# Index columns copied by ScalarE in the first edge stage and the edge GRU, and a later load of target rows in the third layer

## What is computed

```python
h = relu(layernorm(x))
# L0, three times: mean over incoming edges of h[src], at dst
h = relu(h @ W_self.T + b_self + (segment_sum(h[src], dst) * inv_deg) @ W_neigh.T)   # no relu on the third
x = x + h
# L1: h = (mean_dst(h[src]-ea) @ W_O.T + mean_src(h[dst]-ea) @ W_I.T + h @ W_S.T + biases) / 3, batch norm
# L2: messages = segment_sum(h[src] @ W_msg.T + b_msg + emb[type], dst); h = gru_cell(messages, h)
# L3: agg = segment_sum((h @ W.T + b)[dst], src) / deg
```

## Time and profile before

| | |
|---|---|
| median of three runs | 6240.1 us |
| profiled execution | 6218.8 us |
| its span | 6217.1 us |
| mean granted TensorE clock | 0.838 of full |
| busy over the span | PE 75%, PEld 56%, DVE 65%, ACT 47%, POOL 61% |

### The profile page before, as it was taken

The page is one execution under the profiler, slowest core; times in us unless marked ns, Lnnn a source line. Parts: engine busy times, 40 slices in busy tenths (PEclk is TensorE's granted clock), DMA queues, the critical chain, the costliest instruction groups (busy, mean ns, idle before and its releaser), DMA issues. The chain is left out here.

```text
span 6217.1 us, 110999 instructions
## 1 busy us (share of the span) xinstructions
PE 4637.3 (75%) x24481; PEld 3476.5 (56%) x24651; DVE 4013.2 (65%) x15472; ACT 2945.0 (47%) x6694; POOL 3765.4 (61%) x4109
## 2 busy tenths in 40 slices
PE   3886946668998997734756656899999988865564
PEld 1564634445686686624655444786666654544564
DVE  4875844444684685634237757769999989974431
ACT  0585744443583584433211100548888875544200
POOL 0466666660570470075747750758888878867687
PEclk7997966679999998855878989559999999985687
DMA  3454545558888887845766679544544445534554
GB/s 98 144 193 126 180 151 178 182 174 308 298 289 305 308 291 255 291 143 158 256 207 123 125 135 253 151 140 170 172 170 171 170 149 156 164 98 147 133 101 73
DMA packets 744937, 1140.21 MB, mean 183 GB/s; under 512 B 106431, under 2 KB 427341, under 8 KB 744420
## 3 DMA queue, kind: packets, MB, share of 16 engines
q1 hardware_dynamic: 571170, 898.39, 44.3%
q0 software_dynamic: 137600, 175.02, 13.2%
q10 hardware_dynamic: 36000, 64.94, 2.8%
HBM read 703.65 MB, written 456.37 MB: 187 GB/s over the span
## 5 line engine op out<-in xcount | busy, mean ns | idle before, releaser
L1078 POOL DMA_INDIRECT G_x<-node_table,G_idx x400 | 396.8, 992 | 625.2 <-ACT G_idx L1064 504.2
L1413 DVE TENSOR_SCALAR B_S<-B_krow,dst_keys,inverse_degree_dst 127x125 f32<-127x125 f32 x800 | 222.2, 345 | 387.1 <-DMA B_krow<-keys_dst 385.1
L1078 POOL DMA_INDIRECT G_V<-layer_rows,G_idx x400 | 384.6, 962 | 123.8 <-issue 114.0
L1107 PE MATMUL bank<-first_last_indicators,G_V 125*128 (+1 forms) x1600 | 272.7, 293 | 180.7 <-DVE G_V L1721 180.6
L1425 PE MATMUL bank<-B_S,B_V 127*128 127x125 f32 x2000 | 310.9, 304 | 125.3 <-DVE B_S L1413 107.2
L1886 POOL DMA_INDIRECT node_table<-H_out,H_idx x200 | 322.7, 1614 | 130.2 <-issue 67.9
L1107 PEld LDWEIGHTS bank<-first_last_indicators,G_V 125*128 125x128 f32 x1600 | 276.8, 261 | 184.8 <-issue 130.1
L1886 POOL DMA_INDIRECT out<-O_out,O_idx x200 | 312.1, 1561 | 89.7 <-issue 58.3
L1425 PEld LDWEIGHTS bank<-B_S,B_V 127*128 127x128 f32 x2000 | 270.8, 210 | 154.3 <-DVE B_S L1413 85.7
L2128 PE MATMUL bank<-O_r,O_eq 125*125 125x128 f32 x1592 | 228.7, 314 | 142.4 <-ACT O_out L2140 107.5
L2701 ACT ACTIVATE P_h<-P_x,P_nb,P_rs 128x128 f32<-128x128 f32 x784 | 320.2, 479 | 0.0
(11 more groups left out here) (480 smaller groups left out, 15084.7 us busy)
## 6 DMA issues: line engine op xcount, KB each, us to landing
P_x<-node_table SPq DMA_DIRECT2D x196, 512.0 KB
B_V<-values SPq DMA_DIRECT2D x250, 256.0 KB, 3.1
B_krow<-keys_dst SPq DMA_DIRECT2D x250, 250.0 KB, 3.9
BN_g<-node_table SPq DMA_DIRECT2D x195, 256.0 KB
out<-P_out SPq DMA_DIRECT2D x195, 256.0 KB
node_table<-G_xg SPq DMA_DIRECT2D x97, 512.0 KB
values<-G_V SPq DMA_DIRECT2D x150, 256.0 KB
layer_rows<-A_a SPq DMA_DIRECT2D x100, 256.0 KB, 3.0
```

Source lines behind the costliest of these rows:

```text
L1078: pool.indirect_dma_start(out=rows[u][:, c, :], out_offset=None, in_=table, in_offset=bass.IndirectOffsetOnAxis(ap=idx[u][:, c:c + 1], axi ...
L1107: last = nc.tensor.matmul(m.bank[7][:, bass.ds((i * TILE + c) * 2, 2)], V[0:EP, c, :], m.ind[0:EP, bass.ds(i * TILE + c, 1), :].rearrange( ...
L1413: last = nc.vector.tensor_scalar(S[u][:, cs], krow[u][0:EP + 2, cs], m.kext[0:EP + 2, t], m.inv_d[0:EP + 2, t], ALU.is_equal, ALU.mult)
```

## The change

At the first edges GpSimd's two column copies are gone; ScalarE makes them, those of the first four groups ahead of its loop and those of group i + 4 right after the root of group i. In the edge GRU GpSimd's copy is gone as well; ScalarE makes it, six groups ahead, into eight slots instead of four, and GpSimd's loop body is written out for eight groups instead of four. In the third layer SP's load of xd moves from three groups ahead to one, behind V, krow and h of group i + 3, and waits for x1 of group i - 3 instead of that of group i - 1.

```diff
@@ edges_start, gpsimd
                     f.after(s_h, i - 4)
                     f.landed(s_xo, i - 4, u)
-                    copy_index(nc, m.i_src, idx_s, s_is, i, u)
                     gather(pool, f, idx_s, s_is, i, u, a["x"], xs_whole, s_gs)
-                    copy_index(nc, m.i_dst, idx_d, s_id, i, u)
                     gather(pool, f, idx_d, s_id, i, u, a["x"], xd_whole, s_gd)
@@ edges_start, scalar
                     if has(i):
                         ln.root(f, i, u)
+                        if has(i + 4):
+                            scalar_index(nc, m.i_src, idx_s, s_is, i + 4, u)
+                            scalar_index(nc, m.i_dst, idx_d, s_id, i + 4, u)
...
+                for g in range(4):
+                    scalar_index(nc, m.i_src, idx_s, s_is, g, g)
+                    scalar_index(nc, m.i_dst, idx_d, s_id, g, g)
                 pads_clear(P, act)
-                sweep(act, 0, n, n + 3, body, back=8, ahead=0, special=0)
+                sweep(act, 0, n, n + 3, body, back=8, ahead=4, special=0)
@@ third_layer, sync
                     f.after(s_m, i - 4)
                     sp.dma_start(h[u][:], turned(m.HDa, i)).then_inc(s_h[u], 16)
-                    f.after(s_x1, i - 4)
-                    sp.dma_start(xd_whole[u][:], edge_rows(m.XD, i)).then_inc(s_x[u], 16)
 
                 def body(i, u, has):
                     f = Flow(sp, has)
                     if has(i + 3):
                         load(f, i + 3, (u + 3) % 4)
+                    if has(i + 1):
+                        w = (u + 1) % 4
+                        Flow(sp, has, m).after(s_x1, i - 3)
+                        sp.dma_start(xd_whole[w][:], edge_rows(m.XD, i + 1)).then_inc(s_x[w], 16)
@@ gru
-        agg, idx = P.slots("agg", [128, EG]), P.slots("idx", [128, TILE], I32)
+        agg, idx = P.slots("agg", [128, EG]), P.slots("idx", [128, TILE], I32, count=8)
@@ gru, gpsimd
                     g = Flow(pool, has, m)
-                    next_index(nc, g, m.i_dst, idx, s_i, i + 3, u + 3, s_x)
                     if has(i + 2):
                         g.after(s["x2"], i - 2)
-                        gather(pool, g, idx, s_i, i + 2, (u + 2) % 4, m.XG, x_whole, s_x)
-
-                sweep(pool, -3, n, n + 4, body, back=7, ahead=3, special=0)
+                        half = (u + 2) % 8 // 4 * 4
+                        gather(pool, g, idx[half:half + 4], s_i, i + 2, (u + 2) % 4, m.XG, x_whole, s_x)
+
+                sweep(pool, -2, n, n + 4, body, unroll=8, back=7, ahead=2, special=0)
@@ gru, scalar
                         f.after(s["nb"], i - 2)
+                        if has(i + 6):
+                            nc.scalar.activation(idx[(u + 6) % 8][:], m.i_dst[:, bass.ds((i + 6) * TILE, TILE)], ACT.Copy).then_inc(s_i, 1)
                         f.after(s["T"], i - 4)
...
-                sweep(act, 0, n, n + 4, body, unroll=8, back=9, ahead=0, special=0)
+                for g in range(8):
+                    nc.scalar.activation(idx[g][:], m.i_dst[:, bass.ds(g * TILE, TILE)], ACT.Copy).then_inc(s_i, 1)
+                sweep(act, 0, n, n + 4, body, unroll=8, back=9, ahead=6, special=0)
```

## The result

| | before | after |
|---|---|---|
| median of 4 runs each, us | 6236.68 | 6130.43 |
| lowest to highest | 6230.12 to 6243.64 | 6122.01 to 6134.77 |
| profiled execution (span) | 6218.8 (6217.1) | 6134.77 (6133.1) |

The changed kernel takes 0.9828 of the time, 95% interval 0.9811 to 0.9845: 106 us less.

What follows compares the result with a forecast made beforehand. Bounds: GpSimd in first edges and edge GRU, with VectorE nearly full there; SP's xd wait and a two-group loop in the third layer. -60 - 49 - 9 = -118 us, 6240.1 - 118 = 6122 us; range 6096 to 6158.

Steps and rivals of the forecast that it cites:

- First edges, -60: First edges: without GpSimd's column copies, gathers start 1.26 us apart across groups; -60 us, bounds -52 to -66.
- the four gaps of 1.67 us: First edges: four gaps between gathers with no copy in them make 5.5 us, and stay.
- the loop of TensorE and ScalarE: First edges, next in line as bound: products, transposes, ScalarE copies, products; at worst 8.0 us a group, under 10.05.
- The rival that the 0.81 us are the wait's: First edges: the wait remains with or without a copy; -20 in place of -60, 6162 us; chance 0.04.
- Third layer, -49: Third layer: SP's xd wait goes, DMA engines bound next at 374 GB/s, 4.17 us a group; -49 us.
- The bound from the 395 GB/s of the earlier trace: Third layer: at the 395 GB/s its own start shows for 4 us, 3.95 us a group, -59 us.
- Edge GRU, -9: Edge GRU: the copy's 0.19 us leaves GpSimd's round, 46 groups, -9 us; bounds -27 and +9.
- some 0.7 us of that is slack: Edge GRU: of VectorE's 0.88 us four-column operation L2478, ending just as GpSimd's subtraction ends, some 0.7 us is slack.
- so the 0.19 is not taken back by it: Edge GRU: VectorE has 0.7 us of slack in the round, so it doesn't take back the 0.19 us.
- The collision that I had as a rival for +32: Edge GRU: each round a gather collides with VectorE, +0.9 us a round; +32 in place of -9, 6163 us; chance 0.05.
- My sign of being wrong, gathers above 1.1 us on average: Edge GRU: gathers longer than 1.1 us on average would show the prediction wrong.
- The other rivals: Third layer gains little, -15 (0.10); first edges bound by TensorE, -30 (0.07); slower, xd too late, 6255 us (0.02).

Runs made afterwards that it cites:

- first_edges_gpsimd_ahead: Kernel before, with GpSimd still copying the first edges' index columns, but one group ahead; on the second chip 6839.9 and 6841.5 us, ratios 1.0116 and 1.0109.
- gru_d_first: Changed kernel, with GpSimd's h - n moved ahead of the power rs in the edge GRU; 6832.3 us on the second chip, ratio 1.0089 against the kernel before.

## Why the prediction was right or wrong, point by point

The time, 6130.4 us, is 8 us from the forecast of 6122. That it is so near is in part luck, since two errors partly cancel: 14 us too little expected of the first two parts, 29 too much of the third.

- **First edges, -60: right in mechanism, 6 us short.** The stage gave 65.6, the bound of -66. The term that was mis-sized is the 5.5 us of the four gaps of 1.67 us, which I said would stay; they went with the copies. ScalarE's 100 copies cost nothing that can be seen, and the loop of TensorE and ScalarE was no bound: TensorE still waits for ScalarE, 77.8 us in 20 groups. That is so on the first chip only; on the second the stage got longer.
- **The rival that the 0.81 us are the wait's** was half right: 0.65 of them are the wait's, as first_edges_gpsimd_ahead shows, but the wait goes with the copy, so nothing was left of it. The rival had the wait remain without a copy; the earlier trace rows rightly spoke against that.
- **Third layer, -49: right in mechanism, 9 us short.** The wait at xd went, and the transfers became a limit, as said, if not the only one; but the stage moves 402 GB/s, not the 374 of the first layer, and that rate is the term that was mis-sized. The bound from the 395 GB/s of the earlier trace rows was the nearer row: it gives 3.95 us a group and -59; 3.92 and -57.6 were measured. I had preferred the longer average; but the first layer has TensorE busy 152 of 160 us, so its rate may be what it asks for and not what the DMA engines give. The Trainium skill, "DMA: Bandwidth & Descriptors", Where 436 GB/s comes from, has the HBM side bind at about 358 GB/s, a figure it gets by sharing a stack's rate between two cores; this kernel runs on one core, and its 402 over 160 us is above it.
- **TensorE's clock**: I took its 3.8 us a group at a granted 0.86. With the stage faster the clock was 1.00 and TensorE took 132.85 / 40.8 = 3.26. Nothing hung on it here.
- **Edge GRU, -9: wrong, +19.9, outside its bounds of -27 to +9.** The step that failed is "some 0.7 us of that is slack", and with it "so the 0.19 is not taken back by it". The 0.88 us of ve are no slack but 0.17 of work and 0.7 that h - n costs VectorE; VectorE was full, and 0.19 us fewer on GpSimd moved h - n from ve onto hnew, which costs 0.6 more. The collision that I had as a rival for +32 is what happened, at 0.51 us a round in place of 0.9, but not as I drew it: I had gathers stretched by the selectors. They were stretched, by 0.29 us a round, but not by those (0.95 us beside them at 5260.69), and the dearest instruction was VectorE's. Its 0.9 us a round was not in the rows either: 1.42 against 0.96 is 0.46, some +12 us for the part in place of +32. The bounds were drawn from gathers alone; they should have held the 1.3 us by which a long operation of VectorE can be held. My sign of being wrong, gathers above 1.1 us on average, was badly chosen: they average 1.12 in the kernel before (223.5 us for 200) and 1.17 after.
- **The other rivals** did not come: the third layer gained in full, first edges met no other bound on this chip, and no x1 waited for its rows (what ended the waits of L1620 was ScalarE's h, L1202, or issue).

## What to carry to other kernels

Where two engines in order go round side by side, one of them full, a removed instruction is not worth its duration: it shifts everything behind it against the other engine. List the operations of the full engine that the other can hold, with what each is held by, and ask which of them the moved instruction will fall on; then try the order, not only the count. And a load that has to wait for a slot belongs behind the loads that don't, or in a slot that has long been free: both brought x1's run in the third layer from over 241 us to about 189.

## What the runs showed of the hardware that I had not expected

- Between a GpSimd copy of 0.20 us and the gather behind it lie 0.81 us if the gather waits for that copy, and 0.16 if it waits for an older one.
- GpSimd's subtraction of 128x500 beside a VectorE operation costs that one 0.7 us (ve, selectors) or 1.3 us (hnew, q), as the table of rounds shows.
- Two full engines can lock into either of two rounds, 8.03 and 8.54 us, and stay in it through a stage of 50 groups, with the same code in that stage (446.3 and 466.7 us).
- Two chips ran the kernel before in 6239 and in 6771 us. On the second, first edges of the changed form were some 90 us slower than the old ones (691 against 601), while the third layer gained there as on the first. The closest kernels to the changed one that ran there, gru_d_first with its long round among them, were 0.4 to 0.9% slower than the kernel before. The gain of 1.7% is that of one chip. On the other the changed kernel itself didn't run; from its stages there, +90 for first edges, -52 for the third layer (300.9 to 249.0) and +20 for the GRU, I estimate some 58 us more, a loss of 0.9%. Why is open.
